# Convolution pairs packed into slots 0 to 8, with the statistics, halo copies, stores, loads and rounding moved to match

## The reference

```python
# layer 0: quantised 3x3 convolution
scale_input = max(abs(gn)) / 128            # over the whole batch
x_q = round(clip(gn / scale_input, -127, 127))
x = x + conv3x3(x_q, w_int8) * (scale_input * scale_weight) + bias
# layer 1: a complex 3x3 convolution over the spectrum
X = rfftn(groupnorm(x)); Y = complex conv3x3(X) + bias
x = x + irfftn(Y)
```

## Time and profile before

| | |
|---|---|
| median of 3 runs | 3781.86 us (3779.63 to 3790.49) |
| the profiled execution | 3767.42 us |
| its span, first to last instruction | 3765.6 us |
| PE busy, PEld busy | 79%, 70% of the span |
| DVE, ACT, POOL busy | 83%, 50%, 40% |
| mean granted TensorE clock | 0.992 of full |
| data moved by DMA | 730.98 MB, mean 194 GB/s |

### The profile page before, as it was taken

How to read it: one execution, slowest core, us unless ns; L and a number is a source line. 1 busy time by engine, 2 the same in 40 slices (tenths; PEclk the granted TensorE clock), 3 DMA queues, 4 the chain that set the end, 5 groups by cost and what they waited for, 6 DMA issues and landing times.

```text
span 3765.6 us, 126495 instructions
## 1 busy us (share of the span) xinstructions
PE 2979.5 (79%) x45732; PEld 2646.9 (70%) x45732; DVE 3117.7 (83%) x5880; ACT 1893.1 (50%) x2799; POOL 1490.4 (40%) x1984
## 2 busy tenths in 40 slices
PE   0000004899999999999999989999999999999998
PEld 0000002788888888888888878888888888888888
DVE  8999994688878888888888878888888888888876
ACT  8999981344444444444444434444444444444443
POOL 4777000344334344343343334333433433333444
PEclk9999999999999999999999999999999999999999
DMA  8767650366666666666666656666666666666655
GB/s 309 241 236 242 236 188 16 118 196 198 198 188 196 197 195 197 194 192 195 199 194 191 195 178 194 194 192 195 192 194 191 196 192 194 193 199 191 198 179 179
DMA packets 630696, 730.98 MB, mean 194 GB/s; under 512 B 76752, under 2 KB 602160, under 8 KB 614736
## 3 DMA queue, kind: packets, MB, share of 16 engines
q1 hardware_dynamic: 482640, 588.71, 48.6%
q10 hardware_dynamic: 147456, 134.28, 12.7%
HBM read 262.58 MB, written 134.22 MB: 105 GB/s over the span
## 4 chain that ended last, share of the span: by engine, by line
PE 50%; SPq 16%; issue 11%; DMA 11%; DVE 9%; ACT 1%; POOL 1%; ACTq 1%; DVEq 0%; POOLq 0%
PE y_ps L985 12%; PE mean_b L1030 10%; SPq L454 9%; PE conv_ps L1017 7%; PE x_ps L972 6%; DMA stack<-xn 5%; PE fin_ps L1004 5%; SPq L376 4%; PE t_ps L963 3%; DMA out<-img 3%; PE conv_ps L1019 3%; DVE scaled L758 2%; DMA img<-in_x 2%; PE fin_ps L999 2%; DVE scaled L759 1%
## 5 line engine op out<-in xcount | busy, mean ns | idle before, releaser
L729 POOL TENSOR_SCALAR eo<-img,norm 128x256 f32<-128x256 f32 x512 | 481.5, 940 | 1502.1 <-PE t_ps L963 1274.2
L985 PEld LDWEIGHTS y_ps<-mix_w,stack 128*128 128x128 f16 x24576 | 787.5, 99 | 158.1 <-DMA stack<-xn 84.6
L985 PE MATMUL y_ps<-mix_w,stack 128*128 128x64 f16 x24576 | 810.4, 194 | 62.4 <-DMA stack<-xn 62.0
L540 ACT ACTIVATE xt<-t_ps 128x512 f32<-128x512 f32 x512 | 305.8, 597 | 910.8 <-PE t_ps L963 802.9
L554 ACT ACTIVATE y_hi<-y_ps 128x512 f16<-128x512 f32 x512 | 305.8, 597 | 535.4 <-PE y_ps L985 534.4
L834 DVE SCALAR_TENSOR_TENSOR img<-conv_ps,cst,img 128x512 f32<-128x512 f32 x512 | 382.3, 747 | 226.9 <-PE conv_ps L1019 226.4
L821 DVE SCALAR_TENSOR_TENSOR xn<-x_ps,norm,xn 128x512 f16<-128x512 f32 x512 | 383.1, 748 | 220.7 <-ACT xn L547 215.6
L1030 PE MATMUL mean_b<-row_mean,img 128*128 128x48 f32 x4096 | 538.2, 275 | 16.6 <-DVE img L834 16.2
L972 PE MATMUL x_ps<-dft,xt 128*128 128x128 f32 x4096 | 543.0, 276 | 0.0
L1030 PEld LDWEIGHTS mean_b<-row_mean,img 128*128 128x128 f32 x4096 | 511.3, 196 | 31.7 <-DVE img L834 31.5
L972 PEld LDWEIGHTS x_ps<-dft,xt 128*128 128x128 f32 x4096 | 499.7, 192 | 0.1
(11 more groups left out here) (134 smaller groups left out, 5138.9 us busy)
## 6 DMA issues: line engine op xcount, KB each, us to landing
stack<-xn SPq DMA_DIRECT2D x2048, 132.0 KB, 2.6
img<-in_x SPq DMA_DIRECT2D x1024, 128.0 KB, 2.8
out<-img ACTq DMA_DIRECT2D x1024, 128.0 KB, 3.0
img<-in_x SPq DMA_DIRECT2D x120, 1024.0 KB, 4.9
halo<-quant SPq DMA_DIRECT2D x192, 193.3 KB, 3.3
halo<-quant SPq DMA_DIRECT2D x64, 169.1 KB, 3.0
row_mean<-table_row_mean SPq DMA_DIRECT2D x1, 768.0 KB, 15.4
spread<-table_spread SPq DMA_DIRECT2D x1, 512.0 KB, 14.4
```

The lines of the kernel that those rows point to most:

```text
L729: nc.gpsimd.tensor_scalar(even, rows[:, :, 0:F], norm[v][:, 2:3], None, ALU.add).then_inc(shift_s, 1)
L985: last = nc.tensor.matmul(y_ps[t % 2][:, g, b, :], stack[:, t % 2, g, first:first + F], mix_w[:, 2 * at + b, g, f, part, :], start=i == 0, ...
```

## The change

The convolution pairs lie earlier: two in each of slots 0 to 4, one in slots 5 and 6, two in slots 7 and 8. They lay one in each of slots 0 to 3 and two in each of slots 4 to 9. The statistics and the border rows' transform come one slot earlier. Rounding is 12 pairs ahead. SP issues halo copies at the head of its slots 0, 4, 8 and 12, in place of the end of slots 2, 6, 10 and 14. A slot stores the pair before its own in place of the one two before, and loads the one two before in place of three before.

```diff
-CONV_OF = [[j] if j < 4 else [2 * j - 4, 2 * j - 3] if j < 10 else [] for j in range(PAIRS)]
+CONV_OF = [[0, 1], [2, 3], [4, 5], [6, 7], [8, 9], [10], [11], [12, 13], [14, 15]] + [[]] * 7
-STATS_AT = 10
-IMAGE_AT = 12
-AHEAD = 10
+STATS_AT = 9
+IMAGE_AT = 11
+AHEAD = 12
...
                 for t in range(PAIRS):
-                    if mix and t >= 3 and ahead:
-                        sp.wait_ge(store_s[(t - 3) % STORES], stored(s, t - 3))
+                    if t in (0, 4) and conv:
+                        halo_rows(s + 1, t // 4 + 2)
+                    if t in (8, 12) and ahead:
+                        halo_rows(s + 2, t // 4 - 2)
+                    if mix and t >= 2 and ahead:
+                        sp.wait_ge(store_s[(t - 2) % STORES], stored(s, t - 2))
                         sp.sem_inc(tick_s, 1)
-                        load_pair(s + 2, u, t - 3)
-                    if later(s, mix) and t < 3 and conv:
-                        sp.wait_ge(store_s[(t - 3) % STORES], stored(s - 1, t + PAIRS - 3))
+                        load_pair(s + 2, u, t - 2)
+                    if later(s, mix) and t < 2 and conv:
+                        sp.wait_ge(store_s[(t - 2) % STORES], stored(s - 1, t + PAIRS - 2))
                         sp.sem_inc(tick_s, 1)
-                        load_pair(s + 1, 1 - u, t + PAIRS - 3)
+                        load_pair(s + 1, 1 - u, t + PAIRS - 2)
                     if runs(mix, conv, t + 3):
                         restack(s, t + 3)
-                    if t in (2, 6) and conv:
-                        halo_rows(s + 1, t // 4 + 2)
-                    if t in (10, 14) and ahead:
-                        halo_rows(s + 2, t // 4 - 2)
...
-                    if mix and t >= 2:
-                        store(s, u, t - 2)
-                    if later(s, mix) and t < 2:
-                        store(s - 1, 1 - u, t + PAIRS - 2)
+                    if mix and t >= 1:
+                        store(s, u, t - 1)
+                    if later(s, mix) and t == 0:
+                        store(s - 1, 1 - u, PAIRS - 1)
...
-            for t in (PAIRS - 2, PAIRS - 1):
-                store(samples - 1, 1, t)
+            store(samples - 1, 1, PAIRS - 1)
```

## The result

The changed kernel is slower. Its median is 3830.9 us (3812.86 to 3841.92, 4 runs), that of the kernel before in the same runs 3786.18 us; the ratio is 1.0112, with a 95% interval of 1.0067 to 1.0158. The forecast was slower, at 3798 us, so the sign is right and about 0.4% of the 1.1% was foreseen. The measured time lies in the wide range, 3750 to 3845, but above the forecast's own, 3790 to 3815; the rival called clearly slower, at 3840, is nearer to it in number.

The account below looks back on a forecast made before the run. SP's issuing was taken to bound the head and PE the tail: +0.5 us over 30 periods is 15, period 30 -1.3, rounding +2.8, in all +16.5 on 3781.86, giving 3798 us; range 3750 to 3845, likeliest case 3790 to 3815.

Parts of the forecast that it names:

- clearly slower: Rival, chance 0.15: late restack costs slots 1 and 2 0.7 us each, SP keeps its store waits; +1.9 a period, 3840 us.
- The head: Stretch of the period that SP sets: slot 10 to slot 1's mix before, 40.5 us; slot 9 to slot 0's after, 38.6.
- the tail: Rest of the period, set by PE: 56.2 us before, 58.6 after, then starting from the mix of slot 0.
- POOL's wait: PE's wait for POOL, at most 1.7 us a period: it goes, but lay inside a stretch SP sets, so gains nothing.
- The wait of the first row means in slot 0: Second convolution pair's row means wait for `layer0_pair` behind the restack: PE stands 1.1 us, bounds 0 and 1.1.
- The store waits: SP's waits for stores in slots 13 and 14, part of 5.5 us a period, lost with the halo ahead.
- SP without waits from slot 9 to slot 0: Sign expected in the profile after: SP has no waits throughout the new head.
- From the last restack to the mix: End of the head, from issue of the last restack to PE's mix: 5.4 us before and after.
- Halo copies, stores, loads and rounding: Halo copies free outside slot 12, stores and loads cost nothing; two more pairs rounded before the lead period cost 2.8 us.
- Period 30: No loads in its head, so POOL's wait counts there: -1.3 us, between 0 and -1.7.
- SP is quick enough: Rival, faster, chance 0.23: SP's steps in the head at 4.7 us or below, store waits vanish; -1.5 a period, 3738 us.
- no change: Rival, chance 0.22: DVE has `layer0_pair` of slot 0 done half of the 1.1 us earlier; -0.1 a period, 3780 us.

## Why the prediction was right, and what was too small in it

*The head is SP's and the tail PE's.* Right, and the two kernels with added matmuls show it: 83 us of PE work are all but free in slots 12 and 14 and cost all of their time in slots 2 and 3. The tail came out at 58.6 us, the sum's own number; in sample 25 slots 1 to 8 are 53.2 of them, as summed.

*POOL's wait buys nothing.* Right. 52.5 us of wait went, and PE's wait for the restack grew by 57.1, from 2.0 to 3.8 us a period where the forecast's sign had about 5. The expectation that it would be worth 40 us once SP has no loads was wrong: the two kernels without loads take the same time.

*The wait of the first row means in slot 0.* It is there, 0.5 us in sample 25 where I had 1.1, as the mix starts a little behind the landing and the zeroing product comes ahead of the row means. The piece from the mix to slot 1 still came out at 5.3 us on average for 5.4, as PE's work in it is some 0.5 us longer than summed; that is luck. The wait was wrong as a loss of its own: with a single pair in slot 0, slot 1 takes the time.

*The head.* This is the term that was mis-sized: 1.9 us were to be saved, 1.1 were. Of the 0.8 that is missing, 0.6 lie in SP's steps, 1.3 saved for 1.9. The sum had 6.0, 4.9, 6.8, 4.9 and 4.9 in order of time, 27.5 us; they average 6.1, 5.2, 6.4, 5.3 and 4.9, 27.8, in the first profile of the changed kernel and 6.1, 5.3, 6.5, 5.4 and 5.0, 28.3, in the second. The plain steps are what is too small. The 4.9 came from two of the four plain steps of one period; the two left out, from slot 12 to 14, are 2728.62 - 2718.14 = 10.5 us together, and the average of the three from slot 11 on is 5.2 in the kernel before. On the other side that kernel's five steps average 29.1, and 29.4 was set against the sum.

*The store waits.* The sum took those of slots 13 and 14 for gone, and there they are: 0.6 and 0.6 us on average before, 0.2 and 0.0 after. But the one in the first step, which the sum has inside its 6.0, averages 1.1, so the five steps have 1.6 us of such waits for 1.3, and the sign "SP without waits from slot 9 to slot 0" failed. Over the execution they grew from 166.9 to 242.3 us, most of that in the tail, where it costs nothing. One reading in this term was wrong: the 3.0 us of the earlier trace rows count from the start of a transfer's issue, and the sum put them behind both issues of the store, some 0.8 too late. The second transfer lands 3.3 us after its start on average here, and the first step came out as summed.

*From the last restack to the mix.* I took 5.4 from one place; it averages 6.1, and 6.0 in the kernel before. It is wrong by as much in both, so it adds to the length of the period (97.2 for 98.5) and hardly to the difference of +0.5 and +1.28.

*Halo copies, stores, loads and rounding.* Right that they cost nothing together; the kernel with the old convolution places has 0.9989. They did not shorten the whole, as the 1.9 us less in the head had it. The two pairs rounded before the lead period cost 2.8 in the sum and 2.9 in the trace.

*Period 30.* From the last L854 to the end it is 3811.1 - 3714.0 = 97.1 us against 3765.6 - 3671.6 = 94.0. The statistics come one bare slot of 3.6 sooner, so the gain is 0.5 us, where the sum had 1.3.

*The rival "SP is quick enough".* Its condition was a step of 4.7 or less. No step of the head was that short on average. The Trainium skill's rule on interleaving (Perfetto Trace Analysis, section Optimization Strategy) stood on the right side: the change drew PE's work together, the tail grew by 2.4 us, and the head, which lost a convolution pair, shrank by 1.1 only.

*The rival "clearly slower".* 3840 is 9 us from the measured 3830.9, the forecast 33. But slots 1 and 2, which were to lose 0.7 us each, are 7.10 and lose nothing; that SP does not lose its store waits is half true, as above. Its number is near by luck.

*The rival "no change".* Its condition held: the wait of the first row means is half of the 1.1. The piece it stands in came out no shorter, and the head longer than summed.

## What to carry to other kernels

Where two resources take turns to set the pace, look at how much work of the one lies in the time of the other before any wait is removed. A wait that ends inside a stretch that another queue paces is worth nothing, and work that is moved out of such a stretch costs its full price in the other. Added dummy work in one stretch and then in another is a quick test of which of them an engine sets. Moving a transfer to another queue does not help where the transfers delay each other in flight, and what stands behind it on the new queue becomes late. A difference of 1 us in a period of 97 has to be built from averages over many periods; a single period was off by 0.5 us and more in some pieces.

## What the runs showed of the hardware

A wait of PE of 1.1 us, once a period, was followed by half clock in 11 of 31 such slots of the kernel before, and in 9 to 21 of 31 across the kernels here that have it; the most, 20 and 21, are in the two without loads. The slot is 1.6 us longer then. With four matmuls of 512 columns added in that wait, the clock was at full in all 31. It was worth 0.3% by itself. Added work in the waits of the head won nothing, since SP sets the time there.

Issuing one transfer of a restack takes SP 0.60 us as a median and 0.68 on average here, so six transfers in a slot are 4 us, and a plain step of the head is 5. A restack lands 5.1 us after its first issue on average, and after 7.1 to 7.3 where ACT had a halo copy in flight beside it.
